# Cross-attention of a Flamingo block on one core: order of its first loads, of the last split stores and of the next phase's scale

## The chip, the core and the metric

The kernel runs on one core of a Trainium2 chip. The metric is the device time of one execution in microseconds (us); for the kernel before it is the median of three timed runs. Engines: PE (TensorE), DVE (VectorE), ACT (ScalarE), POOL (GpSimd) and SP (SyncE, which here only issues DMAs).

## The reference, cut to what matters

Two gated layers on x of 8 x 256 rows of 512 (2048 rows). Each layer adds a gated cross-attention and then a gated feed-forward part:

```python
x = x + tanh(g_xattn[0]) * L0_xattn(ctx, ctx, layernorm(x), ...)     # long convolution
x = x + tanh(g_ffn[0])   * L0_ffn(layernorm(x), ...)                 # 8 routed experts and a shared one
x = x + tanh(g_xattn[1]) * L1_xattn(layernorm(x), ctx, Wq, Wg, bg, Wkv, Wo)
x = x + tanh(g_ffn[1])   * L1_ffn(layernorm(x), gamma, beta, mu, scale, W1, b1, W2, b2)   # soft MoE

# L1_xattn: feature map f(x) = x + 1 if x > 0 else exp(x), 16 heads of 32
q = f(query @ Wq.T); gate = sigmoid(query @ Wg.T + bg); k, v = f(ctx @ Wk.T), ctx @ Wv.T
out = ((q @ (k.T v)) / (q . sum(k) + eps) * gate) @ Wo.T
# L1_ffn begins with, for each batch of 256 rows:
x_ln = (x - mean) / sqrt(var + eps) * gamma + beta
x_n  = x_ln / max(norm(x_ln), 1e-12) * scale        # the row's scale: scale / max(norm, 1e-12)
```

## The kernel before, in words

The program is a chain of phases, each a block in which all engines run their own instruction list; a phase ends when every engine has come to its end, and SP's end waits until all its stores have landed. Products in near-fp32 precision are made from fp16 halves: an operand is split into `hi` (an ACT copy) and `lo` (a subtraction on DVE or POOL), and each product is three matmuls.

**The routed-expert phase** (`expert_phase`) goes over 39 tiles of 128 gathered rows. PE expands and contracts a tile, DVE copies its result into `e_y` (line 1288), and SP stores it to `expert_rows` (line 1311). Beside that, a "background" splits the soft MoE's `mu` in four quarters of four pieces; SP stores a piece's halves from `mu_q` to `mu_split` (line 1319). In SP's list the stores lag five tiles behind, so after the loop over tiles come five more stores of `e_y`, and after them what is left of the background, three stores of `mu_q`.

**The cross-attention phase** (`xattn_phase`) goes over four chunks of 512 rows (four tiles each). The order of the work is a list `schedule` of steps (chunk, operation, number), walked by each engine, which does its own part of each step:

- TC: transpose a tile of context rows (`rows_ahead`, loaded ahead for chunk 0), split into `a_ct`.
- K, V, KF: keys and values of a tile, 12 matmuls each. DVE clamps K's result (`a_low`), ACT takes its exp, DVE adds the two to `a_feat`; ACT splits it. V is split from PSUM by ACT (`a_v_hi`) and DVE (`a_v_lo`, line 1742).
- CB: DVE adds a tile's two gathered expert rows (`a_y`, gathered by POOL) to the stored rows `a_x` (lines 1684 and 1687) and takes their statistics. NA, NB: layer norm into `a_xn`. TX: transpose and split it (`a_xt`, lines 1804, 1598, 1735).
- Q, G, QF: queries and gate; SM, SS: key-value summary (`a_kv`) and its split (lines 1761, 1645, 1766); AT: attention; OUT: output projection, added into `a_x` (line 1786) and stored.
- P: split one piece of the soft MoE's W1 or W2 (ACT copies it, POOL subtracts, ACT's queue stores it and loads the next).

At the start PE does TC, all of K and V, then TX, then Q. The others walk the list `beside`: four TC, CB mixed into the first two K, V, KF, then NA, NB, TX, and then the last two K, V, KF. All steps use eight PSUM banks in turn, so a step waits until the bank's user eight before it has been read.

In the last chunk six steps are mixed into the queries and gates: `first_norm`, the layer norms of the soft MoE's first batch (N1a to N2b on `rows_ahead`), then N3a (ACT: squares with row sums, line 1610, and a square root, line 1612) and N3b (DVE: the row's scale `s_rs`, lines 1725 to 1730, which waits for N3a). `mixed(a, b)` places step i of a list of n at (i + 0.5) / n and sorts both by that, so the places depend on the lengths of both lists.

SP's list at the phase's begin is a loop over the five weight loads (wk, wv, wq, wg, wo; 1 MB each) with the row loads put between them:

```python
for n in range(5):
    if n == 1:
        load_rows(0)
    if n == 3:
        load_next(0)
    sp.dma_start(halves[n]..., xw_split[n]).then_inc(w_loaded[n], 16)
```

`load_rows(c)` loads 1 MB of `a_x`; `load_next(c)` waits until the chunk's context has been transposed and then loads the next chunk's context (1 MB) and rows. At the same time ACT's queue loads three pieces for P and POOL gathers eight times 256 KB of `a_y`.

Of the kernel before, what the change touches and what calls it, by code (L numbers as in the profile page):

```python
# [22 lines left out]
KD = D // P  # L23
CH = 4 * P
NCH = T // CH
# [27 lines left out]
def mixed(a, b):  # L53

    at = [((i + 0.5) / len(a), 0, o) for i, o in enumerate(a)] + [((i + 0.5) / len(b), 1, o) for i, o in enumerate(b)]
    return [o for _, _, o in sorted(at, key=lambda v: v[:2])]
# [500 lines left out]
TILES = (2 * T + E * (P - 1)) // P  # L557
# [488 lines left out]
def expert_phase(nc, k, w, xn, y_out, mu, mu_split, ctx, xw, xw_split):  # L1046
# [7 lines left out]
    with phase(nc) as st:  # L1054
# [250 lines left out]
        @block.sync  # L1305
        def _(sp):
            LAG = 5

            def store(n):
                sp.wait_ge(y_done, n + 1)  # L1310
                sp.dma_start(y_out[n * P:(n + 1) * P, :], y[:, n % U, :]).then_inc(stored[n % U], 16)

            def load_mu(j, c):
                sp.dma_start(mu_in[:, j % 2, c, :], mu_d[:, c, j * D:(j + 1) * D]).then_inc(mu_loaded[j % 2], 16)

            def store_mu(j, c):
                sp.wait_ge(MU["hi"], j * KD + c + 1)
                sp.wait_ge(MU["lo"], j * KD + c + 1)
                sp.dma_start(mu_out[j, c], mu_q[:, :, c, :]).then_inc(MU["stored"], 16)

            def background(n):
                if 1 <= n <= 2 * KD:
                    load_mu(*divmod(n - 1, KD))
                for j, c in ((quarter_at(n, 13 + c), c) for c in range(KD)):
                    if j is not None:
                        store_mu(j, c)
                        if j + 2 < NJ:
                            load_mu(j + 2, c)

            for n in range(TILES):  # L1330
                u = n % U
                if n == TILES // 2:

                    sp.wait_ge(w.x1s_stored, NCH * 16)
                    sp.dma_start(k.ahead.home[:, :, :], ctx.rearrange("(c k p) d -> p (c k) d", p=P, k=4)[:, 0:4, :]).then_inc(k.ahead.ctx_loaded, 16)
                sp.wait_ge(gathered[u], (n // U + 1) * 16)
                if n >= U:

                    sp.wait_ge(expanded, n - U + 1)
                sp.dma_start_transpose(xt[:, u], rows[:, u, :]).then_inc(turned[u], 16)  # L1340
                if n >= LAG:
                    store(n - LAG)
                background(n)
            for n in range(TILES - LAG, TILES):
                store(n)
            for n in range(TILES, FIRST + PERIOD * (NJ - 1) + 13 + KD):
                background(n)
            sp.wait_ge(MU["stored"], NJ * KD * 16)
            for u in range(U):
                sp.wait_ge(stored[u], TILES // U * 16)  # L1350
# [10 lines left out]
def xattn_phase(nc, k, x1s, y_rows, ctx, xw_split, bg_cols, x3, w1, w1_split, w2, w2_split, gamma, beta, scale):  # L1361
# [3 lines left out]
    with phase(nc) as st:  # L1365
# [53 lines left out]
        def projections(c, first, second, last, count):  # L1419

            return [(c, op, n) for n in range(count) for op in (first, second, last)] if c < NCH else []
# [6 lines left out]
        beside = (ops(0, "TC", 4) + mixed(ops(0, "CB", 4), key(0) + key(1)) + ops(0, "NA", 1) + ops(0, "NB", 1)  # L1428
                  + ops(0, "TX", 4) + key(2) + key(3))
        schedule = []  # L1430
        first_norm = [(0, op, 0) for op in ("N1a", "N1b", "N2a", "N2b", "N3a", "N3b")]
        for c in range(NCH):
            schedule += mixed(projections(c, "Q", "G", "QF", KD),
                              [o for n in range(4) for o in ((c + 1, "TC", n), (c + 1, "CB", n))] if c + 1 < NCH else first_norm)
            schedule += ops(c + 1, "NA", 1) + ops(c, "SM", 4) + ops(c, "SS", 2) + ops(c + 1, "NB", 1)
            schedule += mixed(projections(c + 1, "K", "V", "KF", 4), ops(c, "AT", 2 * KD))
            schedule += mixed(ops(c, "OUT", 4), ops(c + 1, "TX", 4))
        parts = iter(range(PARTS))
        steady = [o for at in schedule for o in ([at, (0, "P", next(parts))] if at[1] == "QF" or at[1] == "AT" and at[2] % 2 else [at])]
# [26 lines left out]
        def _(sp):  # L1466
# [10 lines left out]
                load_rows(c + 1)  # L1477

            sp.dma_start(bg[:, :], bg_cols).then_inc(small_loaded, 16)
            for n in range(5):  # L1480
                if n == 1:
                    load_rows(0)
                if n == 3:
                    load_next(0)
                sp.dma_start(halves[n].rearrange("p q k d -> p (q k d)"), xw_split[n]).then_inc(w_loaded[n], 16)
            for c in range(NCH):
                if 0 < c < NCH - 1:
                    load_next(c)
                if c == NCH - 2:

                    sp.wait_ge(c_turned, NCH * 4)
                    sp.wait_ge(stored, c * 4 * 16)
                    sp.dma_start(ah.x_ln, x3_d[:, 0:2, :]).then_inc(AS["x_loaded"], 16)
                    for dst, src in ((ah.gam, gamma), (ah.bet, beta), (ah.scl, scale)):
                        sp.dma_start(dst[:, :], src.partition_broadcast(P)).then_inc(AS["small"], 16)
                for t in range(4):
                    sp.wait_ge(out_read, c * 4 + t + 1)
                    sp.dma_start(x3_d[:, c * 4 + t, :], x2[:, c % X_BUFS, t]).then_inc(stored, 16)
# [1043 lines left out]
```

## Time and profile before

| | |
|---|---|
| median of three runs | 1770.28 us (1766.94 to 1773.11) |
| profiled execution: own time, span | 1764.81 us, 1762.9 us |
| PE busy | 1565.1 us (89% of the span) |
| DVE, ACT, POOL busy | 1092.9, 757.6, 513.8 us |
| mean granted TensorE clock | 0.957 of full speed |
| PE busy from 700 to 800 us, granted clock | 77.6 us of 100, 0.88 |
| PE busy from 1000 to 1100 us, granted clock | 73.1 us of 100, 0.86 |

All times within the program count from the start of the span. The routed-expert phase ends, and the cross-attention begins, at about 734 us; the soft MoE begins at about 1084 us. A busy PE is read together with its clock: a matmul of 512 columns follows the one before by 0.22 us at full clock and by 0.43 us at half.

### The profile page before, as it was taken

To read this page: it belongs to the slowest core of one execution; us is meant where nothing else is said; L and a number is where in the kernel's file an instruction comes from. 1 tells how busy PE (TensorE), PEld (TensorE's weight loads), DVE (VectorE), ACT (ScalarE), POOL (GpSimd) and SP (SyncE) were. 2 spreads that over 40 slices of the span, in tenths; PEclk is the share of its full clock that TensorE was granted. 3 is DMA by queue.
4 is the path that set the end of the run, shared out by engine and by line. 5 is a ranking of instruction groups with operands and counts; after the bars stand their busy time and mean duration, and the time that the engine had idled before them with its cause. 6 is when DMAs were issued, how large, how long until landed. Compare 5 with 4: busy or idle time off the path is not lost. (4 is left out here: it accounts for less than half of the span.)

```text
span 1762.9 us, 27544 instructions
## 1 busy us (share of the span) xinstructions
PE 1565.1 (89%) x9484; PEld 908.1 (52%) x9484; DVE 1092.9 (62%) x2221; ACT 757.6 (43%) x1393; POOL 513.8 (29%) x428
## 2 busy tenths in 40 slices
PE   4989948999799999679898876889999999999997
PEld 3778833444356566435454442545555555555554
DVE  7998845335623333268685864766676767575663
ACT  5443214333123333134343451656564656566462
POOL 0657824333324444234342331120202010101101
PEclk7999969999999999889999997989999999999999
DMA  9545544645596887552434215624250505142241
GB/s 206 145 118 151 160 149 134 199 146 153 172 222 168 242 210 193 196 197 77 151 90 163 70 64 217 220 68 84 49 118 20 125 18 113 38 93 57 63 89 44
DMA packets 293579, 228.83 MB, mean 130 GB/s; under 512 B 197778, under 2 KB 241298, under 8 KB 291170
## 3 DMA queue, kind: packets, MB, share of 16 engines
q1 hardware_dynamic: 244912, 156.73, 34.7%
q10 hardware_dynamic: 39298, 40.54, 8.0%
q0 software_dynamic: 9264, 30.15, 5.6%
q8 instruction: 66, 1.08, 0.3%
q14 instruction: 39, 0.32, 0.1%
HBM read 125.58 MB, written 54.87 MB: 102 GB/s over the span
## 5 line engine op out<-in xcount | busy, mean ns | idle before, releaser
L2127 POOL TENSOR_TENSOR s_h_lo<-s_h,s_h_hi 128x512 f16<-128x512 f32 x32 | 37.0, 1155 | 550.9 <-DVE s_h_hi L2329 550.9
L2347 PE MATMUL s_ring<-w_mu,s_xt_hi 128*128 128x512 f16 x256 | 99.5, 389 | 7.0 <-DVE s_xt_lo L2250 3.8
L1275 DVE TENSOR_TENSOR e_h<-e_up,e_silu 128x352 f32<-128x352 f32 x39 | 20.4, 524 | 137.0 <-ACT e_silu L1220 137.0
L2255 DVE TENSOR_REDUCE s_top<-s_lg 128x1 f32<-128x512 f32 x64 | 43.9, 686 | 92.7 <-ACT s_lg L2169 92.5
L2348 PE MATMUL s_ring<-w_mu,s_xt_hi 128*128 128x512 f16 x256 | 99.3, 388 | 0.0
L2349 PE MATMUL s_ring<-w_mu,s_xt_lo 128*128 128x512 f16 x256 | 99.1, 387 | 0.0
L2347 PE MATMUL s_acc<-w_w,s_g_hi 128*128 128x512 f16 x256 | 97.1, 379 | 0.2
L2347 PE MATMUL s_ring<-w_w,s_xt_hi 128*128 128x512 f16 x256 | 97.0, 379 | 0.0
L2348 PE MATMUL s_ring<-w_w,s_xt_hi 128*128 128x512 f16 x256 | 97.0, 379 | 0.0
L2349 PE MATMUL s_ring<-w_w,s_xt_lo 128*128 128x512 f16 x256 | 97.0, 379 | 0.0
L2349 PE MATMUL s_acc<-w_w,s_g_lo 128*128 128x512 f16 x256 | 97.0, 379 | 0.0
L2348 PE MATMUL s_acc<-w_w,s_g_hi 128*128 128x512 f16 x256 | 97.0, 379 | 0.0
L524 PE MATMUL ring<-prod_hi,toep 128*128 128x288 f16 x320 | 91.9, 287 | 4.9 <-DVE terms L438 4.7
L303 POOL TENSOR_TENSOR prod_lo<-prod,prod_hi 128x2304 f16<-128x2304 f32 x15 | 69.2, 4612 | 86.3 <-ACT prod_hi L339 86.3
L525 PE MATMUL ring<-prod_lo,toep 128*128 128x288 f16 x320 | 91.8, 287 | 0.0
L526 PE MATMUL ring<-prod_hi,toep 128*128 128x288 f16 x320 | 91.8, 287 | 0.0
L1220 ACT ACTIVATE e_silu<-e_gate 128x352 f32<-128x352 f32 x39 | 18.1, 463 | 149.1 <-PE e_up L1150 149.1
L2175 ACT ACTIVATE s_dt<-s_ring,s_slot_low 128x256 f32<-128x256 f32 x128 | 59.5, 470 | 52.4 <-DVE s_dq L2277 52.1
L2332 DVE TENSOR_TENSOR s_g_lo<-s_ring,s_g_hi 128x512 f16<-128x512 f32 x64 | 43.5, 690 | 58.2 <-ACT s_g_hi L2206 58.2
L339 ACT ACTIVATE prod_hi<-prod 128x2304 f16<-128x2304 f32 x16 | 34.0, 2128 | 92.9 <-DVE prod L409 92.9
L2169 ACT ACTIVATE s_lg<-s_ring,s_rs 128x512 f32<-128x512 f32 x64 | 43.7, 683 | 69.4 <-PE s_ring L2349 68.3
L1126 POOL DMA_INDIRECT e_rows<-normed_rows,slot_token x39 | 38.1, 976 | 121.6 <-DMA e_xt<-e_rows 118.8
(387 smaller groups left out, 4780.8 us busy)
## 6 DMA issues: line engine op xcount, KB each, us to landing
expert_rows<-e_y SPq DMA_DIRECT2D x39, 256.0 KB, 2.8
a_part_in<-in_L_ffn_W ACTq DMA_DIRECT2D x32, 256.0 KB, 3.2
w_split<-a_part_q ACTq DMA_DIRECT2D x32, 256.0 KB, 2.5
w_w<-w_split SPq DMA_DIRECT2D x8, 1024.0 KB, 21.9
toep<-ssm_split ACTq DMA_DIRECT2D x14, 512.0 KB, 5.2
stage<-in_L_ffn_gate_w SPq DMA_DIRECT2D x8, 704.0 KB, 4.4
stage<-in_L_ffn_up_w SPq DMA_DIRECT2D x8, 704.0 KB
xattn_w_split<-e_part_q ACTq DMA_DIRECT2D x20, 256.0 KB
```

What stands on the lines that cost most here:

```text
L303: nc.gpsimd.tensor_tensor(prod_lo[:, u].rearrange("p k e r -> p (k e r)"), prod[:, u, :], prod_hi[:, u].rearrange("p k e r -> p (k e r)"), ...
L524: nc.tensor.matmul(out, w_hi, hi, start=(n == 0), stop=False)
L525: nc.tensor.matmul(out, w_hi, lo, start=False, stop=False)
L526: last = nc.tensor.matmul(out, w_lo, hi, start=False, stop=(n == m))
L1126: nc.gpsimd.indirect_dma_start(rows[:, n % U, :], None, xn, bass.IndirectOffsetOnAxis(ap=k.slot_token[:, n:n + 1], axis=0)).then_inc(gathe ...
L2169: A(lg[:, t, j * D:(j + 1) * D], ring[:, bank, :], ACT.Copy, scale=rs[:, t:t + 1]).then_inc(S["lg_out"], 1)
L2175: last_ = A(dt[:, n % 2, e, :], ring[:, bank, e * N:(e + 1) * N], ACT.Exp, bias=slot_low[:, n % 4, e:e + 1], accum_out=slot_sum[:, 2 * n + ...
L2255: V.tensor_reduce(top[:, t, j:j + 1], lg[:, t, j * D:(j + 1) * D], AX.X, ALU.max).then_inc(S["top_done"], 1)
L2332: V.tensor_tensor(g[1][:, n % G_BUFS, :], ring[:, bank, :], g[0][:, n % G_BUFS, :], ALU.subtract).then_inc(S["g_lo"], 1)
L2347: mm(out_, a[0], b_[0], start=first, stop=False)
L2348: mm(out_, a[0], b_[1], start=False, stop=False)
L2349: return mm(out_, a[1], b_[0], start=False, stop=last_)
```

## The change

Three edits. In `expert_phase`, SP issues the rest of the background (three stores of `mu_q`) ahead of the last five stores of `e_y`. In `xattn_phase`, SP issues wk and wv first; it then waits until wk has landed and issues the rows; waits until wv has landed and issues wq and wg; waits until the four tiles of chunk 0 have been combined and issues the next chunk's context and rows; and then wo. And N3b is taken out of `first_norm` and put behind the AT steps of the last chunk; `first_norm` now has five steps to mix in.

```diff
                 if n >= LAG:
                     store(n - LAG)
                 background(n)
+            for n in range(TILES, FIRST + PERIOD * (NJ - 1) + 13 + KD):
+                background(n)
             for n in range(TILES - LAG, TILES):
                 store(n)
-            for n in range(TILES, FIRST + PERIOD * (NJ - 1) + 13 + KD):
-                background(n)
...
-        first_norm = [(0, op, 0) for op in ("N1a", "N1b", "N2a", "N2b", "N3a", "N3b")]
+        first_norm = [(0, op, 0) for op in ("N1a", "N1b", "N2a", "N2b", "N3a")]
...
             schedule += mixed(projections(c + 1, "K", "V", "KF", 4), ops(c, "AT", 2 * KD))
+            schedule += [(0, "N3b", 0)] if c + 1 == NCH else []
             schedule += mixed(ops(c, "OUT", 4), ops(c + 1, "TX", 4))
...
-            for n in range(5):
-                if n == 1:
-                    load_rows(0)
-                if n == 3:
-                    load_next(0)
+            def load_weights(n):
                 sp.dma_start(halves[n].rearrange("p q k d -> p (q k d)"), xw_split[n]).then_inc(w_loaded[n], 16)
+            load_weights(0)
+            load_weights(1)
+            sp.wait_ge(w_loaded[0], 16)
+            load_rows(0)
+            sp.wait_ge(w_loaded[1], 16)
+            load_weights(2)
+            load_weights(3)
+            sp.wait_ge(combined, 4)
+            load_next(0)
+            load_weights(4)
```

The line numbers of the cross-attention's instructions grow by 9 in the changed kernel (L1742 becomes L1751), those of SP's first loads by less; the work of every engine is otherwise the same.

SP at the end of the routed experts, before: the last tiles' stores (L1311) and the split stores (L1319).

```order
L1340 DMA_TRANSPOSE e_xt<-e_rows 128x8x128
L1311 DMA expert_rows<-e_y 128x512
L1319 DMA mu_split<-mu_q 256x1x512
L1311 DMA expert_rows<-e_y 128x512 x5
L1319 DMA mu_split<-mu_q 256x1x512 x3
L36 UNCONDITIONAL_BRANCH
```

The same place in the changed kernel:

```order
L1340 DMA_TRANSPOSE e_xt<-e_rows 128x8x128
L1311 DMA expert_rows<-e_y 128x512
L1319 DMA mu_split<-mu_q 256x1x512 x4
L1311 DMA expert_rows<-e_y 128x512 x5
L36 UNCONDITIONAL_BRANCH
```

Three split stores have moved ahead of five row stores, and a row store is now the phase's last.

SP at the begin of the cross-attention, before (wk to wo are the weights, `a_x` the rows, `rows_ahead` the next context):

```order
L1479 DMA a_bg<-in_bg_cols 128x4
L1485 DMA a_wk<-xattn_w_split 128x4096
L1471 DMA a_x<-after_shared 128x4x512
L1485 DMA a_wv<-xattn_w_split 128x4096
L1485 DMA a_wq<-xattn_w_split 128x4096
L1476 DMA rows_ahead<-in_ctx 128x4x512
L1471 DMA a_x<-after_shared 128x4x512
L1485 DMA a_wg<-xattn_w_split 128x4096
L1485 DMA a_wo<-xattn_w_split 128x4096
```

And in the changed kernel:

```order
L1480 DMA a_bg<-in_bg_cols 128x4
L1483 DMA a_wk<-xattn_w_split 128x4096
L1483 DMA a_wv<-xattn_w_split 128x4096
L1472 DMA a_x<-after_shared 128x4x512
L1483 DMA a_wq<-xattn_w_split 128x4096
L1483 DMA a_wg<-xattn_w_split 128x4096
L1477 DMA rows_ahead<-in_ctx 128x4x512
L1472 DMA a_x<-after_shared 128x4x512
L1483 DMA a_wo<-xattn_w_split 128x4096
```

wv has moved ahead of the first rows, and wg ahead of the next context and rows.

ACT in the last chunk, before, from N3a (L1610, L1612) to the split of the key-value summary (L1645):

```order
L1610 ACTIVATE a_y,s_squares<-rows_ahead 128x512 x2
L1612 ACT_TABLE_LOAD
L1612 ACTIVATE s_l<-s_squares 128x2
L1627 ACT_TABLE_LOAD
L1627 ACTIVATE a_low_exp<-a_low 128x512
L1636 ACTIVATE a_gate<-a_ring,a_bg 128x512
L1642 ACTIVATE a_q_hi<-a_feat 128x512
L1582 ACTIVATE a_part_q<-a_part_in 128x512
L1574 DMA w_split<-a_part_q 256x1x512
L1567 DMA a_part_in<-in_L_ffn_W 128x512
L1645 ACTIVATE a_kv_hi<-a_kv 128x1024 x2
```

And in the changed kernel (L1636 is now the exp, L1645 the gate, L1619 and L1621 are N3a, L1654 the split):

```order
L1636 ACTIVATE a_low_exp<-a_low 128x512
L1645 ACTIVATE a_gate<-a_ring,a_bg 128x512
L1619 ACTIVATE a_y,s_squares<-rows_ahead 128x512 x2
L1621 ACT_TABLE_LOAD
L1621 ACTIVATE s_l<-s_squares 128x2
L1651 ACTIVATE a_q_hi<-a_feat 128x512
L1591 ACTIVATE a_part_q<-a_part_in 128x512
L1583 DMA w_split<-a_part_q 256x1x512
L1576 DMA a_part_in<-in_L_ffn_W 128x512
L1654 ACTIVATE a_kv_hi<-a_kv 128x1024 x2
```

With five steps to mix in instead of six, N3a itself has moved behind the last exp and the last gate, and one table load is gone.

## Rows read from the trace of the kernel before

**Rows 1.** Waits of PE, 700 to 1100 us: total us, times, longest.

```profile
PE a_ring L1798 <- DVE a_kv_lo L1766: 12.4, 4, 6.8
PE a_ring L1798 <- DMA a_wv<-xattn_w_split: 6.3, 1, 6.3
```

**Rows 2.** Timeline of SP's queue: start us, length us, queue, line, transfer.

```profile
712.47 16.72 SPq L1311 DMA_DIRECT2D expert_rows<-e_y  x5
729.29 1.86 SPq L1319 DMA_DIRECT2D mu_split<-mu_q  x3
...
734.71 1.74 SPq L1485 DMA_DIRECT2D a_wk<-xattn_w_split  x1
736.50 0.43 SPq L1471 DMA_DIRECT2D a_x<-after_shared  x1
```

**Rows 3.** Waits of SP, 728 to 736 us: total us, times, longest.

```profile
SPq L36 <- DMA mu_split<-mu_q: 2.0, 1, 2.0
```

**Rows 4.** Timeline of PE: start, length, line, [idle before it, releaser].

```profile
753.35 0.58 PE L1798 MATMUL a_ring<-a_wv,a_ct_hi 128*128 128x512 f16 x1 [6.33 <-DMA a_wv<-xattn_w_split]
...
772.91 1.91 PE L1804 MATMUL a_ring<-ident,a_xn 128*128 128x128 f32 x16
779.79 0.39 PE L1798 MATMUL a_ring<-a_xt_hi,a_wq 128*128 128x512 f16 x1 [4.96 <-DVE a_feat L1676]
```

**Rows 5.** Timeline of DVE at the cross-attention's begin.

```profile
750.41 0.75 DVE L1684 SCALAR_TENSOR_TENSOR a_x<-a_y,mix,a_x 128x512 f32<-128x512 f32 x1 [2.66 <-DMA a_x<-after_shared]
...
758.20 0.69 DVE L1742 TENSOR_TENSOR a_v_lo<-a_ring,a_v_hi 128x512 f16<-128x512 f32 x1 [5.53 <-ACT a_v_hi L1621]
...
774.18 2.48 DVE L1735 TENSOR_TENSOR a_xt_lo<-a_ring,a_xt_hi 128x512 f16<-128x512 f32 x4 [1.27 <-ACT a_xt_hi L1598]
```

**Rows 6.** Timeline of DVE in the last chunk.

```profile
1042.29 0.17 DVE L1725 TENSOR_SCALAR s_l<-s_l 128x2 f32<-128x2 f32 x1 [4.06 <-ACT s_l L1612]
...
1044.23 0.69 DVE L1676 SCALAR_TENSOR_TENSOR a_feat<-a_ring,a_low_exp 128x512 f32<-128x512 f32 x1 [1.31 <-ACT a_low_exp L1627]
...
1076.96 0.75 DVE L1786 SCALAR_TENSOR_TENSOR a_x<-a_ring,tanh_gates,a_x 128x512 f32<-128x512 f32 x1 [4.28 <-PE a_ring L1800]
```

**Rows 7.** Timeline of ACT in the last chunk.

```profile
1038.86 0.63 ACT L1610 ACTIVATE a_y<-rows_ahead 128x512 f16<-128x512 f32 x1 [1.25 <-POOL rows_ahead L1550]
...
1042.28 1.28 ACT L1627 ACT_TABLE_LOAD   x1
1043.57 0.63 ACT L1627 ACTIVATE a_low_exp<-a_low 128x512 f32<-128x512 f32 x1
...
1046.49 2.25 ACT L1645 ACTIVATE a_kv_hi<-a_kv 128x1024 f16<-128x1024 f32 x2 [0.38 <-DVE a_kv L1761]
```

**Rows 8.** DMA issues, 728.5 to 734.3 us: KB each, median us to landing.

```profile
mu_split<-mu_q SPq DMA_DIRECT2D x3, 256.0 KB, 2.6
```

**Rows 9.** DMA issues, 700 to 800 us: KB each, median us to landing.

```profile
expert_rows<-e_y SPq DMA_DIRECT2D x7, 256.0 KB, 2.0
...
a_wk<-xattn_w_split SPq DMA_DIRECT2D x1, 1024.0 KB, 7.7
a_wv<-xattn_w_split SPq DMA_DIRECT2D x1, 1024.0 KB, 16.2
```

**Rows 10.** Tile mu_q, 690 to 830 us: ns min/median/max, first and last start.

```profile
L1112 POOL TENSOR_TENSOR mu_q<-mu_in,mu_q x4: 1149/1156/1602, 695.4 to 701.4; 128x512 f16<-128x512 f32 x4
```

**Rows 11.** DMA queues, 734.3 to 742.5 us: packets, MB, share (q1 is SP's).

```profile
q1 hardware_dynamic: 364, 1.21, 39.0%
```

**Rows 12.** The same for 742.5 to 750.4 us (q0 carries POOL's gathers).

```profile
q0 software_dynamic: 448, 1.50, 49.3%
q1 hardware_dynamic: 502, 1.30, 43.9%
```

**Rows 13.** Tile a_x, 690 to 830 us: its two loads' time to landing.

```profile
DMA to landing us min/median/max: 13.9/18.3/22.7
```

**Rows 14.** Timeline of POOL in the last chunk.

```profile
1037.30 2.68 POOL L1550 TENSOR_TENSOR rows_ahead<-rows_ahead 128x512 f32<-128x512 f32 x2
```

## The prediction

> **What bounds the kernel now.** The waits of PE from 700 to 1100 us come first, because PE is busy for most of the span and only a stretch where it stands idle can give something back. Two of them matter here [rows 1]: 6.3 us for the weights wv, once, and 12.4 us in four waits for `a_kv_lo`, the longest 6.8. Then SP's timeline at the change of phases [rows 2]: five row stores are issued up to 729.19 (712.47 + 16.72), three split stores behind them up to 731.15, and SP then waits 2.0 us for the last of these to land [rows 3]; the block ends with it, at 733.15, and the first load follows at about 734.
>
> At the cross-attention's begin, read PE and DVE side by side. PE starts V of tile 0 at 753.35, when wv has landed; the transposes of the normed rows start at 772.91, that is 19.56 us later, and the first query at 779.79, behind a wait of 4.96 us for DVE [rows 4]. DVE combines tile 0 from 750.41, when the rows `a_x` have landed, then stands idle for 5.53 us until V's split at 758.20; its split of the normed rows begins at 774.18 after 1.27 idle [rows 5]. So wv ends the first wait, and from 758.20 to the first query the order of DVE's list sets the time.
>
> In the last chunk DVE stands still for 4.06 us until 1042.29, when N3a has given its root, and then 1.31 us more until 1044.23 for the last exp [rows 6]. ACT shows why both come together [rows 7]: the squares of N3a start at 1038.86, the root's end is followed by a table load at 1042.28, the exp at 1043.57, and the split of the key-value summary only at 1046.49. The longest `a_kv_lo` wait of PE, 6.8 us, is the end of this row of work.
>
> **Split stores ahead of the last rows: 2.2 us less.** What they store has long been made: POOL's last piece of `mu_q` starts at 701.4 and takes at most 1.6 us [rows 10], and the split stores need 1.86 us of issue in a gap of SP that lasts until 712.47 [rows 2]. So they delay no row store. The phase now ends with the landing of the last row store. It is issued just before 729.19, at about 728.9 (an estimate: a split store's share of the 1.86 us is 0.6, a row store is shorter), and a row store lands 2.0 us after its issue [rows 9], at 730.9, where a split store takes 2.6 [rows 8] and ended the phase at 733.15. Gain 733.15 - 730.9 = 2.2 us. The ends: nothing, if another engine's end holds the block; 2.3 at best. The Trainium skill ("DMA: Bandwidth & Descriptors", Anatomy of one DMA) gives 2.0 us fixed and 436 GB/s per DMA, by an estimate 2.6 us for 256 KB whichever store it is; by that the gain would be 1.7 us. The row of this very store decides for 2.2.
>
> **Order of the first loads: 3.8 us less.** Times here stay on the clock of the old trace. wk is issued at 734.71 and lands 7.7 us later [rows 2, 9], at 742.4, as before: what was queued behind it on SP's queue did not hold it. Behind it came the rows, issued at 736.50 and landed 13.9 us later [rows 13], at 750.4, and wv at about 753.2. The two now change places. For wv, SP's queue moved 1.30 MB in the 7.9 us beside 1.50 MB of gathers [rows 12]; at that rate its 1.05 MB need 6.4 us and land at 748.8; at wk's own pace, 1.21 MB in 8.2 us with the start included [rows 11], at 749.5; if it merely takes the rows' old place, at 750.4. The rows are issued when wk has landed, while wv still has 6 us to go, so the queue does not run dry; the total ahead of both is what it was, so they land at 753.2 at the latest.
>
> DVE therefore starts tile 0 at 753.2. Between 750.41 and 758.20 it worked 758.20 - 5.53 - 750.41 = 2.26 us [rows 5], so it comes to V's split at 755.5. V's result needs 758.20 - 753.35 = 4.85 us from PE's start [rows 4, 5]; from 750.4 at the latest that is 755.2, in time. From 758.20 to 755.5 are 2.7 us, and the chain behind it (three more tiles, the norm) is DVE's own. The transposes may start 19.56 us after V: at 768.5 from a start at 748.9, which lies ahead of the norm, so that the 1.27 us of idle before 774.18 go too: 4.0 us. With wv at 750.4 the transposes start at 770.0 and 2.9 us are gained. I take 3.8, near the upper end, since the measured rates say 748.8 to 749.5. The ends: all of PE's 6.3 us, and a loss of 9.2 (rival two).
>
> The added waits on SP hold wq and wg until wv has landed: they are wanted by the first query, 26 us later. The next context and rows, held until tile 3 is combined, are issued at the latest when the norm ends, 772.91 - 2.7 = 770.2; with wk's 7.7 us the context is there by 777.9, and PE wants it only when the first query, which starts at 776.0, has run. Behind them stands only wo, wanted a chunk's attention later. I cost these at nothing; uncovered, each us late would be one us of PE.
>
> **N3b later, and N3a with it: 3.0 us less.** Moving N3b alone would gain nothing: with DVE's wait gone, its next step still needs the last exp, and that stood behind N3a on ACT. But with five steps instead of six to mix in, N3a falls behind the last exp and gate. Between its root and the summary's split there were 1046.49 - 1042.28 = 4.21 us [rows 7]: table load, exp, gate, query copy, part copy. Only the two copies are left, at the 0.63 us of such an ACT step [rows 7] some 1.3 us: 2.9 us less. N3a's start is set by POOL, which ended at 1037.30 + 2.68 = 1039.98 [rows 14], and its order is unchanged; the norms' steps stand one query step later on DVE now, which may shift POOL by a few tenths either way. I take 3.0; the ends are nothing, and 3.4 with those tenths in its favour (PE's whole 6.8 us would need the copies gone too). N3b's three small instructions, under 0.7 us from 1042.29 on, now lie behind the attention, ahead of the output's additions on DVE. There DVE waits 4.28 us for PE before 1076.96 [rows 6], which covers them; uncovered they would cost 0.7. The soft MoE uses the scale only later.
>
> **Sum.** 2.2 + 3.8 + 3.0 = 9.0 us; the three places lie one behind the other on the path, and what follows each starts by semaphores, so it shifts whole. From the profiled execution's 1764.81 that gives 1755.8. The runs' median, 1770.28, lies 5.5 above it; the same 9.0 off the median give 1761.3 us. About 0.3% (5.3 us) is what a measurement of this kernel tells from no change.
>
> **Rivals.** One: the rows now end the wait that wv ended. They take 13.9 us to land [rows 13]; counted from their new issue at 742.5 that is 756.4, which with 2.26 us is 758.7: no gain at all from the order. For it speaks that gathers still took 1.50 MB of the queue's time; against it that their bytes and wv's are bounded. Then 2.2 + 3.0 = 5.2 are left: 1765.1 us. Two, on the other side: the rows come later still, at the 22.7 us that the second load of `a_x` took [rows 13], at 765.2. Break-even for them alone is 756.0 (758.20 - 2.26); DVE would lose 9.2, and the sum is a loss of 4.0 us: 1774.3. It is slower than before from 761.2 on, by over 0.3% from 766.5. Against it: the 22.7 us were spent behind five other loads. Three: the third edit only turns the wait round, because N3a now stands ahead of the last query copy and the summary's split on the same engine; it gives nothing if POOL ends 2.9 us later than 1039.98. Then 6.0 are left: 1764.3. Four: the first edit does not do what it says, because the block's end hangs on another engine; 6.8 left, 1763.5.
>
> **How the numbers follow.** The forecast gets 0.65, since each term rests on a wait that the trace names; rival one 0.13, two 0.04, three 0.10, four 0.08. Faster by over 0.3% means below 1765.0: of these cases 0.61, 0.05, 0, 0.07 and 0.07, together 0.80. Slower by over 0.3% is 0.03, half of rival two and some scatter; 0.17 is left for the same. Range: low, all terms at their better ends (2.3 + 6.3 + 3.4) off the median and the 3.3 us that the fastest run lies under it, 1755; high, rival one and the 2.8 us that the slowest run lies above, 1768.
>
> **What would show it.** Right: SP's end no longer waits for `mu_split`, and PE's first transpose comes about 2 us earlier; PE's wait for wv falls from 6.3 us to 2 to 3.5, while DVE's first wait for `a_x` grows to about 5; the first query starts some 33.6 us after wk's landing instead of 37.4 (779.79 - 742.4); DVE's idle before N3b is gone, and PE's longest wait for `a_kv_lo` is near 3.8 us. Wrong: DVE waits for `a_x` past 756 on the old clock; PE waits for the next context or for wq; ACT's summary split does not come within 2 us of N3a's root.

## The result and the profile after

The changed kernel takes 1756.92 us in the median of five runs (1753.38 to 1761.46), the kernel before 1768.60 beside it: a ratio of 0.9929, 95% interval 0.9907 to 0.9951. In a second comparison it was 0.9931 (0.9913 to 0.9950). That is some 12 us faster, more than the 9.0 forecast; 1761.3 us and the range of 1755 to 1768 were on record, and the time lies in the range.

The profiled execution of the changed kernel was the slowest of its five: 1761.46 us, span 1759.6, mean granted clock 0.954. Against the profiled one of before (1764.81, span 1762.9, 0.957) it is only 3.3 us better, so the two are read stretch by stretch. SP's timeline at the change of phases comes first (start us, length us, queue, line, transfer), beside [rows 2]:

```profile
709.21 2.54 SPq L1319 DMA_DIRECT2D mu_split<-mu_q  x4
714.65 16.70 SPq L1311 DMA_DIRECT2D expert_rows<-e_y  x5
734.22 0.33 SPq L1480 DMA_DIRECT2D a_bg<-in_bg_cols  x1
734.60 0.43 SPq L1483 DMA_DIRECT2D a_wk<-xattn_w_split  x1
735.08 0.42 SPq L1483 DMA_DIRECT2D a_wv<-xattn_w_split  x1
739.89 0.38 SPq L1472 DMA_DIRECT2D a_x<-after_shared  x1
743.78 0.32 SPq L1483 DMA_DIRECT2D a_wq<-xattn_w_split  x1
```

The split stores now lie in SP's gap, and the issue of the last row store ends at 731.35 (714.65 + 16.70). SP's waits at that place name `mu_split` no more [rows 3]:

```profile
SPq L1350 <- DMA expert_rows<-e_y: 1.7, 2, 1.1
```

The waits of PE, 700 to 1100 us (total us, times, longest), answer to [rows 1]:

```profile
PE a_ring L1807 <- DVE a_kv_lo L1775: 9.9, 4, 3.3
...
PE a_ring L1813 <- DVE a_xn L1710: 5.2, 1, 5.2
...
PE a_ring L1813 <- PEq L36: 4.0, 1, 4.0
...
PE a_ring L1807 <- DMA a_wk<-xattn_w_split: 2.1, 1, 2.1
```

The wait for wv has gone altogether. In its place PE waits 5.2 us for the normed rows, a wait that did not exist before. The longest wait for `a_kv_lo` fell from 6.8 to 3.3 us. The timelines of PE and of DVE show both places (start, length, [idle before it, releaser]); PE first, to compare with [rows 4]:

```profile
740.01 0.59 PE L1807 MATMUL a_ring<-a_wk,a_ct_hi 128*128 128x512 f16 x1 [2.11 <-DMA a_wk<-xattn_w_split]
...
767.76 3.41 PE L1813 MATMUL a_ring<-ident,a_xn 128*128 128x128 f32 x16 [5.17 <-DVE a_xn L1710]
775.65 0.61 PE L1807 MATMUL a_ring<-a_xt_hi,a_wq 128*128 128x512 f16 x1 [4.48 <-DVE a_feat L1685]
```

DVE, to compare with [rows 5, 6]:

```profile
752.10 0.75 DVE L1693 SCALAR_TENSOR_TENSOR a_x<-a_y,mix,a_x 128x512 f32<-128x512 f32 x1 [6.91 <-DMA a_x<-after_shared]
...
754.28 0.67 DVE L1751 TENSOR_TENSOR a_v_lo<-a_ring,a_v_hi 128x512 f16<-128x512 f32 x1
...
1039.06 0.69 DVE L1685 SCALAR_TENSOR_TENSOR a_feat<-a_ring,a_low_exp 128x512 f32<-128x512 f32 x1 [0.70 <-ACT a_low_exp L1636]
...
1044.95 2.58 DVE L1775 TENSOR_TENSOR a_kv_lo<-a_kv,a_kv_hi 128x1024 f16<-128x1024 f32 x2 [0.84 <-ACT a_kv_hi L1654]
1068.07 0.16 DVE L1734 TENSOR_SCALAR s_l<-s_l 128x2 f32<-128x2 f32 x1
```

DVE now waits for the rows once and then comes to V's split (754.28) without a stop, where it had stood for 5.53 us. In the last chunk no wait for N3a is left; N3b lies at 1068.07. ACT, to compare with [rows 7], has N3a behind the last exp and the last gate (1038.40 and 1039.03), no second table load, and the summary's split 1.41 us behind the root (1043.86 - 1042.45) where it had been 4.21:

```profile
1038.40 0.63 ACT L1636 ACTIVATE a_low_exp<-a_low 128x512 f32<-128x512 f32 x1 [0.91 <-DVE a_low L1678]
1039.03 0.69 ACT L1645 ACTIVATE a_gate<-a_ring,a_bg 128x512 f32<-128x512 f32 x1
1039.61 0.62 ACT L1619 ACTIVATE a_y<-rows_ahead 128x512 f16<-128x512 f32 x1
...
1040.95 1.28 ACT L1621 ACT_TABLE_LOAD   x1
1042.25 0.20 ACT L1621 ACTIVATE s_l<-s_squares 128x2 f32<-128x2 f32 x1
...
1043.86 2.00 ACT L1654 ACTIVATE a_kv_hi<-a_kv 128x1024 f16<-128x1024 f32 x2 [0.37 <-issue]
```

To compare kernels whose phases begin at other times, each profile was cut at the starts of PE's work: the end of the last row store's issue to PE's first transpose ("gap"); that transpose to K, to V and to the first query; from the first query to the last chunk's ("middle": three chunks); from the last chunk's query to its attention ("last"); from there to the next phase ("out"). All in us, worked out from the PE and SP timelines of each run:

```
kernel                gap    K      V      query   middle   last   out    span
before               5.17   8.20  18.99   45.43   237.32   32.06  34.64  1762.9
changed              2.91   5.75  10.03   41.39   242.46   28.43  32.36  1759.6
e1_stores            2.92   5.75  18.02   45.17   237.97   32.04  34.61  1765.2
e2_loads             5.18   5.75  10.02   40.82   236.68   32.03  34.61  1761.0
e3_scale             5.17   6.78  18.70   45.76   235.77   28.48  34.61  1760.7
e5_order_only        5.17   5.79   9.93   41.28   240.03   32.04  34.52  1763.9
e6_hold_only         5.17   5.83  18.11   45.09   239.12   32.05  34.53  1766.0
e7_n3b_only          5.18   7.27  19.44   46.49   238.39   32.03  34.62  1770.3
e8_n3a_only          5.18   5.78  17.86   44.89   238.07   28.74  34.26  1764.3
e9_best              2.91   5.76   9.72   36.62   240.63   28.31  34.63  1758.3
e10_again (changed)  2.92   5.77  10.84   41.49   237.28   28.43  32.35  1756.7
e13_third (changed)  2.91   5.74   9.58   41.53   234.34   28.48  34.64  1755.6
e12_parts_late       2.92   5.41   9.37   39.95   240.65   28.44  34.59  1762.4
e11_best2            2.92   5.40  10.47   36.10   240.23   28.15  34.99  1754.0
```

In the profiled pair the change takes 2.26 us off the gap, 4.04 off the first query's way, 3.63 off the last chunk's; another 2.28 is gone from the last outputs. The middle gives 5.14 back, the routed experts ahead 2.16 and the phases behind 1.61: together the 3.3 us by which the spans differ. The middle's 5.14 was the first thing to clear up.

### The profile page after: what moved, and what is told of

Its sections match the earlier page's. It is cut to its first block and busy times, and to the rows that moved or that the text cites. A ratio compares the mean times of both kernels' runs of the same rounds, so it can differ in the third digit from the quotient of the medians.

```text
span 1759.6 us, 27544 instructions
## 1 busy us (share of the span) xinstructions
PE 1572.1 (89%) x9484; PEld 913.1 (52%) x9484; DVE 1091.7 (62%) x2221; ACT 756.3 (43%) x1392; POOL 512.9 (29%) x428
## 3 DMA queue, kind: packets, MB, share of 16 engines
q1 hardware_dynamic: 244912, 156.73, 34.7%
## 5 line engine op out<-in xcount | busy, mean ns | idle before, releaser
L2341 DVE TENSOR_TENSOR s_g_lo<-s_ring,s_g_hi 128x512 f16<-128x512 f32 x64 | 43.5, 689 | 58.7 <-ACT s_g_hi L2215 58.7
```

Source lines behind the costliest of these rows:

```text
L2341: V.tensor_tensor(g[1][:, n % G_BUFS, :], ring[:, bank, :], g[0][:, n % G_BUFS, :], ALU.subtract).then_inc(S["g_lo"], 1)
```

## The experiments

**Each edit alone.** e1: the stores; e2: the loads with SP's waits; e3: N3b behind AT, `first_norm` of five steps. Core of the three edits, one fence:

```diff
+            for n in range(TILES, FIRST + PERIOD * (NJ - 1) + 13 + KD):     # e1
+                background(n)
             for n in range(TILES - LAG, TILES):
                 store(n)
...
+            load_weights(0); load_weights(1); sp.wait_ge(w_loaded[0], 16)   # e2
+            load_rows(0); sp.wait_ge(w_loaded[1], 16)
+            load_weights(2); load_weights(3); sp.wait_ge(combined, 4)
+            load_next(0); load_weights(4)
...
+        first_norm = [(0, op, 0) for op in ("N1a", "N1b", "N2a", "N2b", "N3a")]   # e3
+            schedule += [(0, "N3b", 0)] if c + 1 == NCH else []
```

> Only the first edit: the three split stores ahead of the last five row stores. Theory (the three terms lie in series and add): from the end of the last row store's issue to the first transpose of the cross-attention 5.1 us become 2.9, and the time falls by 2.3 us (ratio 0.9987). Rival (the edits only pay together, because the earlier begin just moves the wait for wk and wv): the gap is 2.9 us as well, but the stretch from the first transpose to the first query grows by the same 2.3 us and the time stays (1.000).

> Only the second edit: the order of the first loads with its waits. Theory: from the first transpose to the first query 45.4 us become 41.4, and the time falls by 4.0 us (0.9977); wk lands 5.3 us after its issue, as in the whole change, and not 7.7. Rival (wk's early landing in the whole change came from the earlier begin, when the stores' traffic had gone): wk takes 7.7 us again, the stretch is about 43.8 and the time falls by 1.6 (0.9991).

> Only the third edit: five steps mixed in, N3b behind the attention. Theory: from the last chunk's first query to its first attention 32.1 us become 28.4, and the time falls by 3.6 us (0.9980). Rival (the shorter idle of PE also keeps its clock for the output projections that follow): in addition the stretch from that attention to the next phase's first transpose falls from 34.6 to 32.4 us, and the time by 5.9 (0.9967).

Measured: 0.9983 (0.9971 to 0.9995), 0.9978 (0.9963 to 0.9992) and 0.9974 (0.9962 to 0.9986). In the table each edit changes its own stretch, and the others no more than they scatter: e1 the gap by 2.25, e2 the first query by 4.6, e3 the last chunk by 3.58 us. Apart from the middle the first query scatters most: with the old order it came 44.9 to 46.5 us after the first transpose (before, e1, e3, e6, e7, e8), with the new order and nothing else moved there 40.8 to 41.5 (changed, e2, e5, e10, e13); the two means lie 4.2 apart. The rivals fall: in e1 the way to the first query is not longer (45.17), in e2 wk landed early without the earlier begin (K at 5.75), in e3 the outputs kept their 34.61. The three ratios add up to -0.65%, the whole change measured -0.71 and -0.69%: within these intervals the edits add up.

**N3b alone, N3a in its old place.** A sixth step that does nothing keeps the places of the others.

```diff
+        first_norm = [(0, op, 0) for op in ("N1a", "N1b", "N2a", "N2b", "N3a", "none")]
+            schedule += [(0, "N3b", 0)] if c + 1 == NCH else []
```

> N3b behind the attention, but N3a left at its old place (six places to mix in, the last one empty). Theory (N3a on ACT is what held the last exp, and N3b's wait on DVE stood in its shadow): nothing is gained, the stretch from the last chunk's first query to its first attention stays at 32.1 us, within 0.5, and DVE's wait of 4.06 us becomes a wait for the last exp of about 5.4 us (1.000). Rival (N3b's wait on DVE was the cost, as the change's words say): that stretch falls by 3 us or more (0.998).

Measured 0.9996 (0.9983 to 1.0008), last chunk 32.03 us, as before. DVE's timeline tells why: without N3b it waits for the next thing, the last exp behind N3a on ACT, until the same moment: 27.10 us after the chunk's first query (1050.05 - 1022.95), before 27.12 (1044.23 - 1017.11). The wait was expected at about 5.4 us and took 7.22, because DVE came to it earlier.

```profile
1050.05 0.69 DVE L1677 SCALAR_TENSOR_TENSOR a_feat<-a_ring,a_low_exp 128x512 f32<-128x512 f32 x1 [7.22 <-ACT a_low_exp L1628]
```

So the move that the edit spells out is worth nothing by itself.

**N3a late, N3b not behind the attention** but right ahead of SM:

```diff
+        first_norm = [(0, op, 0) for op in ("N1a", "N1b", "N2a", "N2b", "N3a")]
             schedule += ops(c + 1, "NA", 1) + ops(c, "SM", 4) ...
+            schedule before SM: [(0, "N3b", 0)] if c + 1 == NCH else []
```

> N3a moved behind the last exp and gate as in the change (five steps to mix in), but N3b left ahead of the key-value summary, after the last query step, so that DVE waits there for N3a's root; the other two edits left out. Theory (N3a's place on ACT is the gain, N3b's place only has to stay out of DVE's way): DVE waits for the root some 2 to 2.5 us ahead of the summary's evictions, which then run from 42.9 us on the changed kernel's clock instead of 40.3 to 44.1; ACT's split starts about 1 us later than with the whole edit, and the stretch from the last chunk's first query to its first attention is 29 to 30.5 us, between 28.5 (whole edit) and 32.1 (before). Rival (N3a's place is all): 28.5 us. Rival (N3b's place is all): 32 us.

Measured 0.9975 (0.9963 to 0.9988), last chunk 28.74 us. DVE again waits for the root:

```profile
1044.39 0.17 DVE L1726 TENSOR_SCALAR s_l<-s_l 128x2 f32<-128x2 f32 x1 [2.02 <-ACT s_l L1613]
```

That wait costs PE almost nothing: 28.74 beside 28.48 of e3. So the theory's 29 to 30.5 us failed, and the first rival (N3a's place is all) came within 0.3. DVE's wait lies mostly beside ACT's copies: the summary's split started 26.28 us after the chunk's first query (1046.25 - 1019.97), in e3 25.85. Of the third edit's 3.6 us, 3.3 come from N3a's place on ACT, which changed only because five steps mix in elsewhere than six.

**Order without the waits, and a wait without the order.** e5 issues wk, wv, rows, wq, wg, next context and rows, wo with no wait on SP for a landing or for the combined tiles; e6 keeps the order before but holds the rows, and so wv, until wk has landed.

```diff
+            load_weights(0); load_weights(1); load_rows(0)                  # e5
+            load_weights(2); load_weights(3); load_next(0); load_weights(4)
...
+            load_weights(0); sp.wait_ge(w_loaded[0], 16); load_rows(0)      # e6
+            load_weights(1); load_weights(2); load_next(0); load_weights(3); load_weights(4)
```

> Of the second edit the order alone: wk, wv, rows, wq, wg, next context and rows, wo, all issued at once without SP's waits for wk, wv and the combination; the other two edits left out. Theory (wv's place ahead of the rows is what pays, the waits hold back nothing that matters): from the first transpose to the first query about 41 us, as with the waits, and V starts about 10 us after the first transpose. Rival (holding the rows and later weights back is what makes wk and wv land sooner): V starts at 12 us or later, the stretch is 43 to 45 us.

> Of the second edit the holding back alone: the old order (wk, rows, wv, wq, next context and rows, wg, wo), but the rows are issued only when wk has landed; the other two edits left out. Theory (order pays, not holding): wv still lands behind the rows, V starts 18 to 19 us after the first transpose and the first query about 45 us after it, as before; wk may land anywhere between 5.7 and 8.2 us, since it did so in the old order. Rival (holding pays): wk lands at 5.7 us and the first query comes at 43 us or sooner.

Measured: e5 0.9972 (0.9960 to 0.9983), first query at 41.28 us; e6 1.0006 (0.9992 to 1.0020), 45.09 us. In e5 DVE's first wait for the rows is that of the changed kernel; in e6 PE's wait for wv is longer than in the kernel before:

```profile
752.99 0.75 DVE L1688 SCALAR_TENSOR_TENSOR a_x<-a_y,mix,a_x 128x512 f32<-128x512 f32 x1 [6.94 <-DMA a_x<-after_shared]
```

```profile
752.53 0.58 PE L1803 MATMUL a_ring<-a_wv,a_ct_hi 128*128 128x512 f16 x1 [8.24 <-DMA a_wv<-xattn_w_split]
```

So the order does it, and the runs show neither help nor cost of SP's added waits (40.82 with them in e2, 41.28 without). What each of its two moves is worth, wv ahead of the rows and wg ahead of the next context, was not run by itself.

**The changed kernel again, twice,** unaltered, for the middle's 5.14 us and the outputs' 2.28.

> The changed kernel once more, unaltered, since its one profiled execution was its slowest and the two profiles differ by only 3.3 us where the medians differ by 11.7. Theory (the three edits each shorten their own stretch and the rest is scatter of half-clock stretches in the middle chunks): gap before the first transpose 2.9 us, first query 40.8 to 41.4 us after the first transpose, last chunk's query to output 28.3 to 28.7 us, its end to the next phase 34.3 to 34.7 us (not 32.4), middle chunks' outputs to next queries anywhere among 43.5 and 45.1; ratio 0.993 plus or minus 0.002. Rival (a part of the gain is given back in the middle chunks by the new order): middle chunks again about 5 us longer in sum than in the kernel before, ratio the same.

> The changed kernel a third time, one look. In its two profiles the stretch from the last attention to the next phase takes 32.35 us, in every kernel with one edit and in e12_parts_late, whose last chunk is the same, 34.3 to 34.7 us: there PE waits 3.3 us before the last output products and starts them at half clock, here it waits 2.4 us and stays at full clock. Theory (the fall of the clock hangs on where earlier half-clock stretches lie, which differs from run to run): any of the two values may come, near 34.6 us as likely as 32.4. Rival (the three edits together set it every time): 32.3 to 32.4 us again, and 2.3 us of the whole change's gain are from it.

The gap (2.91 to 2.92), the first query (41.39 to 41.53) and the last chunk (28.43 to 28.48) came out the same three times. The middle did not: 242.46, 237.28, 234.34 us of the very same program, which puts the kernel before, at 237.32, in between. So a loss there is not shown; the scatter of 8 us would hide one of a microsecond or two. The outputs were 32.36, 32.35 and 34.64: either value comes, and no edit owns those 2.28 us. So e10's forecast of 34.3 to 34.7 failed, and so did e13's rival, that the three edits set 32.4 every time; why it is one value or the other is not shown. (e13 is a single run, 1757.36 us beside 1771.80.) PE's work and clock by stretch show what differs between two runs of the same instructions, here one stretch of the middle, from the second chunk's query to its attention, in the first profile of the changed kernel and in e10_again (columns: stretch and its length; busy us of PE, PEld, DVE, ACT, POOL; granted clock; DMA share; GB/s):

```profile
854.72:892.16 37.44, 32.74 (x172) 17.31 (x173) 22.93 (x41) 15.59 (x25) 9.11 (x8) 0.91 0.39 117
```

```profile
855.69:890.43 34.74, 29.80 (x172) 16.32 (x173) 22.77 (x41) 15.70 (x25) 9.12 (x8) 1.00 0.41 126
```

PE is busy 2.94 us longer at a granted clock of 0.91 than at 1.00, and the stretch is 2.70 us longer; the others' work is the same.

**What the rows wait for.** The changed kernel, but ACT issues the three first loads of W1 and W2 pieces (0.79 MB) behind the split of tile 1's V instead of at the phase's begin.

```diff
+                    for part in range(PART_BUFS if (c, n) == (0, 1) else 0):
+                        load_part(part)
...
-            for n in range(PART_BUFS):
-                load_part(n)
```

> The changed kernel with one edit: the three first part loads (0.79 MB on ACT's queue) issued after tile 1's value eviction in place of the phase's begin. Theory (the rows land when all bytes ahead of them have moved): at the 3.05 MB per 7.9 us that the engines moved there, 0.79 MB less is 2.0 us; DVE's first row statistics start about 16 us after the first transpose in place of 17.8, first query about 39.5 us in place of 41.3. Rival (the rows' own queue is the limit, other queues' bytes do not matter): 41.3 us, DVE's start unchanged.

First query at 39.95 us, 1.5 sooner than in the changed kernel's three profiles (2.0 expected), and DVE's first rows 16.31 us after the first transpose (753.86 - 737.55) instead of 17.72 to 17.84. Another queue's bytes do delay the rows, so the theory holds; three quarters of its size came. The time, 0.9928 (0.9906 to 0.9949), can't be told from the changed kernel's.

**Two versions beyond the change.** Since DVE stands for 6.9 us before the rows, e9 gives it the key and value steps of tile 0 and the first of tile 1 before it combines, takes N3a out of the queries, behind the attention, and puts N3b behind the outputs. e11 also loads the pieces late as above and moves POOL's gamma and beta right ahead of SM.

```diff
-        beside = (ops(0, "TC", 4) + mixed(ops(0, "CB", 4), key(0) + key(1)) + ...
+        beside = (ops(0, "TC", 4) + key(0) + key(1)[:1] + CB[:3] + key(1)[1:] + CB[3:] + ...
+        first_norm = [(0, op, 0) for op in ("N1a", "N1b", "N2a", "N2b", "none")]
+            schedule += [(0, "N3a", 0)] if c + 1 == NCH else []     # behind AT
+            schedule += [(0, "N3b", 0)] if c + 1 == NCH else []     # behind OUT
+            schedule += [(0, "N2c", 0)] if c + 1 == NCH else []     # e11: gamma, beta ahead of SM
```

> The whole change, and two steps more: N3a too goes behind the attention on ACT and N3b behind the output's additions on DVE; and at the cross-attention's begin DVE does the first K, V, KF and the second K before it combines the rows, since it stood 6.9 us idle for the rows. Theory (the rows' landing at about 17.8 us after the first transpose now sets DVE's chain, so three small steps done in its wait come off the path; ACT's root and table load came off the summary's split): the first query 39 to 39.5 us after the first transpose instead of 41.4, the last chunk's stretch 27.5 instead of 28.4, the time 2 to 3 us under the changed kernel, ratio to before about 0.992. Rival (PE's transposes or the bank order hold it): both stretches unchanged, ratio 0.993 to 0.9935.

> The kernel of e9_best with POOL's gamma and beta of the last chunk moved right ahead of the softmax step and the three first part loads issued on ACT's queue only after tile 1's value eviction. Theory: the rows land sooner since 0.79 MB less is ahead of them (first query about 35 us after the first transpose, e9_best 36.6) and the last chunk's key-value split no longer waits 3.2 us behind a late part store (query to output about 27.5 us, e9_best 28.3); ratio about 0.990. Rival: neither is what holds, first query 36.6, last chunk 28.3, ratio 0.9915 as e9_best.

e9: 0.9915 (0.9900 to 0.9931), first query at 36.62 us, better than expected, since the first wait for the rows is down to 1.78 us; but the last chunk stayed at 28.31, because a part store on ACT's queue held the summary's split, 3.20 us idle, behind POOL's late half. The row names DVE's summary, but the first two of its four steps, which this split needs, were done at 1038.10; POOL's half ended at 1038.82, and the store was issued right behind it:

```profile
1038.91 0.53 ACTq L1584 DMA_DIRECT2D w_split<-a_part_q  x1
...
1040.14 2.00 ACT L1655 ACTIVATE a_kv_hi<-a_kv 128x1024 f16<-128x1024 f32 x2 [3.20 <-DVE a_kv L1771]
```

e11: 0.9906 (0.9889 to 0.9922), 1753.33 us in the median (1752.01 to 1755.96) beside 1757.76 of the changed kernel in the same comparison: the lowest median of all, though the two intervals overlap. Its first query came at 36.10 (about 35 expected), with no wait of DVE for the rows left. The late store is gone from ACT, and DVE's `a_kv_lo`, which PE waits for, starts 1.03 us sooner after the chunk's first query than in e9 (1035.83 - 1009.91 for 1041.23 - 1014.29); ACT's split is paced by DVE's summary there. Yet the last chunk is only 0.16 us shorter. The rest is lost in `a_kv_lo` itself, in e9 first:

```profile
1041.23 2.36 DVE L1776 TENSOR_TENSOR a_kv_lo<-a_kv,a_kv_hi 128x1024 f16<-128x1024 f32 x2 [0.94 <-ACT a_kv_hi L1655]
```

```profile
1035.83 4.29 DVE L1777 TENSOR_TENSOR a_kv_lo<-a_kv,a_kv_hi 128x1024 f16<-128x1024 f32 x2
```

Its first step took 2.09 us in e11 and 1.22 in e9, 0.87 more. Beside it now ran POOL's gamma and beta, which the edit had put there, and they were slow too: 2.24 us for the steps beside `a_kv_lo`, 1.27 for those just ahead of it. That the two slow each other down is what these rows suggest; no run separates them. Without the 0.87 the chunk would have come out at 27.3 by this estimate, near the 27.5 that was expected and did not come.

## Why the prediction held, step by step

**Split stores, 2.2 forecast, 2.26 measured,** in every kernel with the edit (gap 5.17 or 5.18 to 2.91 or 2.92). The step that set 2.0 us for the row store's landing against 2.6 for the split store's [rows 8, 9] was right: SP issued the last row store at 731.02 and was past its wait for it at 733.07. Some 1.7 us of the gain are the earlier issue, the rest is the shorter landing. The estimate from the Trainium skill ("DMA: Bandwidth & Descriptors", Anatomy of one DMA), 1.7, came out 0.6 too small; that section's figures are a fit to DMAs issued by GpSimd, and these stores are SP's. Why the one store lands sooner (its longer pieces, or that no other store is issued right ahead of it) is not shown. Rival four (another engine ends the block) falls with e1.

**Order of the first loads, 3.8 forecast, 4.0 measured (3.9 to 4.6 over the kernels with the order).** The sum came near, in part by luck: two errors in it nearly cancel.

wv first. "At the measured rates wv lands at 748.8 to 749.5", by "SP's queue moved 1.30 MB in the 7.9 us", failed: wv had landed by 743.78, when SP went past its wait, and wk by 739.89, so wv needed 3.9 us behind wk, not 6.4. When wk (1.05 MB) landed, SP's queue had already moved 1.31 MB, a quarter of wv with it; the other 0.81 MB came in 3.9 us beside 0.65 MB of gathers, 0.21 MB per us where [rows 12] have 0.16. Why that rate was higher is not shown. It did no harm: with wv at 749.5 V's result would have been there at 754.35 (749.5 + 4.85), and DVE came to its split at 754.4 on the old clock (754.28 - 734.26 + 734.36).

The rows were the first error. "They land at 753.2 at the latest" held: DVE started the rows 17.84 us after the first transpose, that is at 752.2 on the old clock (734.36 + 17.84), 1.8 later than before. That is rival one's mechanism, the rows as the next bound, at a price that does not take the gain away: in the six kernels with the old order the first query came 26.4 to 27.2 us after V's start, in the six with the new one and an unchanged `beside` 23.4 to 23.8 after DVE's first rows. Because the rows came a microsecond ahead of their latest, DVE was at V's split 3.82 us sooner after the first transpose (23.84 before, 20.02 now), where the forecast had 2.7.

The second error is "so that the 1.27 us of idle before 774.18 go too". From V's split to the first query only 0.22 us more were gained. The transposes came 5.05 us sooner (33.50 after the first transpose for 38.55), but they now waited for `a_xn`; PE had stood idle for 5.17 us and ran the same 16 transposes at a granted clock of 0.56, in 3.41 us instead of 1.91 [rows 4]:

```profile
767.70:771.20 3.50, 3.41 (x16) 3.20 (x16) 2.67 (x5) 1.79 (x3) 1.10 (x2) 0.56 0.96 333
```

DVE's split followed them tile by tile. It started 1.75 us behind them (769.51 - 767.76), where it had been 1.27, and took 3.02 us (to 771.22 + 1.31) instead of 2.48, so that one us of the 5.05 was lost again:

```profile
769.51 0.69 DVE L1744 TENSOR_TENSOR a_xt_lo<-a_ring,a_xt_hi 128x512 f16<-128x512 f32 x1 [0.53 <-ACT a_xt_hi L1607]
770.36 0.69 DVE L1744 TENSOR_TENSOR a_xt_lo<-a_ring,a_xt_hi 128x512 f16<-128x512 f32 x1 [0.16 <-ACT a_xt_hi L1607]
771.22 1.31 DVE L1744 TENSOR_TENSOR a_xt_lo<-a_ring,a_xt_hi 128x512 f16<-128x512 f32 x2 [0.16 <-ACT a_xt_hi L1607]
```

PE's half clock was no term of the sum. So 3.82 + 0.22 = 4.04 us stand where the forecast had 2.7 + 1.27. Of its signs, "2 to 3.5" us of waiting for wv did not come, PE waited for `a_xn` instead; DVE's wait for the rows grew to 6.91, not to about 5.

The yardstick "33.6 us after wk's landing" was badly chosen. wk landed 8.20 us after the first transpose in the profile of before, but 5.75 in e1, with the same order of loads, and the first query hardly moved with it (45.43 and 45.17). In the changed kernel it came 35.6 us after K's start (775.65 - 740.01), which by that yardstick would be half the gain. "What was queued behind wk did not hold it" does not look right: with the rows issued right behind wk, K started at 8.20, 5.75, 6.78, 7.27 and 5.78 us (before, e1, e3, e7, e8), with the new order or the rows held back at 5.4 to 5.8 in all nine profiles. What held it in three of the five is not shown; the query did not depend on it.

**SP's waits at nothing:** right, by e5.

**The scale, 3.0 forecast, 3.6 measured.** That N3b alone gives nothing was right, by e7, and that N3a's place gives it, by e8. From root to split 2.80 us went (4.21 to 1.41; 2.9 forecast). The rest is the clause "may shift POOL by a few tenths either way": POOL's last half started 19.33 us after the chunk's first query (1037.44 - 1018.11) where it had been 20.19 (1037.30 - 1017.11 [rows 14]), 0.86 sooner, and N3a's root came 0.83 sooner. The upper end of 3.4 was too low by these tenths. The row of POOL after:

```profile
1037.44 2.68 POOL L1559 TENSOR_TENSOR rows_ahead<-rows_ahead 128x512 f32<-128x512 f32 x2
```

N3b's three instructions cost nothing visible: the outputs of e3 took 34.61 us, those of before 34.64.

**The sum.** 2.26 + 4.0 + 3.6 is 9.9 us, 0.9 above the forecast; the medians differ by 11.7 and 12.0. Both intervals (8.7 to 16.4, and 8.8 to 15.4 us) take in 9.9. Whether the remaining 2 us are scatter, or whether the changed kernel meets the shorter outputs of 32.4 us more often, as in two of three profiles (and in none of the eleven others), is open.

## What to carry to other kernels

Read a list of loads from the consumer's side: the one whose use sits first on the path goes first, and what its delay costs is told by the engine that stops next, not by the wait that vanished. When a step is taken out of a list whose places depend on its length, look for the steps that moved because of it; here they brought the gain, and the named step by itself brought none. Look, too, at what a moved step comes to lie beside: e11 took POOL's steps off ACT's way and put them beside DVE's. Judge an edit of a few microseconds by its own stretch of the trace, in several profiles, since whole spans of the same program scattered by more than one edit is worth.

## What the runs showed of the hardware

The scatter of this kernel has steps. The stretch from a middle chunk's attention to the next query was 43.5 or 45.0 to 45.2 us in every profile, in the kernel before too, and one unaltered program showed 45.17, 45.08, 45.18 in one profile and 43.51, 43.51, 43.50 in another. The granted clock of that stretch was 0.89 to 0.96 in those of 45 us (0.89 in e7) and 0.96 to 1.00 in those of 43.5: at 0.96 both lengths occur, so the mean alone does not tell which; that it matters where in the stretch the low clock falls is a guess.

What PE did before shows at the 16 transposes of the first chunk's normed rows. In the eight profiles where it had stood idle for at most 1.71 us ahead of them (the six with the old order, e9 and e11) they ran at full clock, in 1.91 to 2.15 us; in the six where it had stood for 4.0 to 5.5 us they ran at a granted clock of 0.50 to 0.57, in 3.25 to 3.65.

At the end of the last chunk the same matmuls went either way. In the first profile of the changed kernel PE stood idle for 2.42 us and started the last output products at full clock; in e12_parts_late, with the same instructions there, it stood for 3.27 and ran the first eight at half clock:

```profile
1069.45 0.38 PE L1807 MATMUL a_ring<-a_wo,a_a_hi 128*128 128x512 f16 x1 [2.42 <-issue]
1069.67 0.38 PE L1808 MATMUL a_ring<-a_wo,a_a_hi 128*128 128x512 f16 x1
```

```profile
1070.06 0.58 PE L1807 MATMUL a_ring<-a_wo,a_a_hi 128*128 128x512 f16 x1 [3.27 <-issue]
1070.44 0.63 PE L1808 MATMUL a_ring<-a_wo,a_a_hi 128*128 128x512 f16 x1
```

The next product follows after 0.22 us in the one and 0.38 to 0.43 in the other.
